# Beginnings of two attention stages: constant semaphores split, weight waits moved to their readers, bias tables loaded through SyncE's queue

## The reference

```
xn = _layernorm(x)
x = x + _L0_attn_ref(xn, ...) + _L0_ffn_ref(xn, ...)
xn = _layernorm(x)
x = x + _L1_attn_ref(xn, ...) + _L1_ffn_ref(xn, ...)
```

## Time and profile before

| | us |
|---|---|
| median of 3 runs | 2233.71 |
| their range | 2226.56 to 2234.21 |
| the profiled execution's own time | 2224.04 |
| its span, first to last instruction | 2222.4 |
| layer 0's attention, about | 0 to 500 |
| layer 0's feed-forward, about | 500 to 1263 |
| layer 1's attention begins | 1268.6 |

### The profile page before, as it was taken

One profiled execution on the slowest core, in us unless ns is written; L12 is line 12 of the kernel. 1 busy time (PEld: TensorE's weight loads), 2 busy tenths in 40 slices (PEclk: granted clock), 3 DMA queues, 4 the chain that ended last, 5 costly groups with the idle time before them and its releaser, 6 DMA issues. The chain is left out here.

```text
span 2222.4 us, 33910 instructions
## 1 busy us (share of the span) xinstructions
PE 1757.2 (79%) x10759; PEld 1099.7 (49%) x10759; DVE 1127.4 (51%) x2401; ACT 1024.4 (46%) x1356; POOL 1007.0 (45%) x778
## 2 busy tenths in 40 slices
PE   3889889870599999999999738877888888747933
PEld 2455555540487787787787513333433433235510
DVE  4666666537513313313313248877787788447211
ACT  1555555543313322223223118887787888713400
POOL 2443444430234344333433308777687777724212
PEclk8999999985799999999999868999998999969965
DMA  3333333306201101101100153222222222043989
GB/s 103 96 96 94 96 95 91 95 11 211 77 1 47 47 0 47 47 0 47 35 12 28 57 198 93 69 71 71 81 67 76 85 63 52 10 177 141 357 306 329
DMA packets 129732, 204.38 MB, mean 92 GB/s; under 512 B 14303, under 2 KB 84063, under 8 KB 129668
## 3 DMA queue, kind: packets, MB, share of 16 engines
q1 hardware_dynamic: 107896, 163.40, 24.7%
q10 hardware_dynamic: 16096, 20.65, 2.6%
q0 software_dynamic: 5680, 19.57, 2.3%
HBM read 95.96 MB, written 56.69 MB: 69 GB/s over the span
## 5 line engine op out<-in xcount | busy, mean ns | idle before, releaser
L773 POOL TENSOR_TENSOR l_prob<-l_prob,l_bias 128x1024 f32<-128x1024 f32 x192 | 452.3, 2376 | 145.5 <-ACT l_prob L881 144.6
L1336 POOL TENSOR_TENSOR f_hl<-f_full,f_hh 128x512 fp32r<-128x512 f32 x192 | 248.1, 1292 | 439.4 <-DVE f_hh L1378 282.9
L946 DVE CUSTOM_DVE_ANT_0 l_slot<-l_slot,l_bias 128x512 f32<-128x512 f32 x512 | 340.4, 714 | 51.5 <-PE l_slot L1020 50.4
L1378 DVE CAST f_hh<-f_full 128x512 fp32r<-128x512 f32 x128 | 74.9, 585 | 397.7 <-ACT f_full L1357 396.2
L884 ACT ACTIVATE l_prob<-l_prob 128x1024 f32<-128x1024 f32 x256 | 271.0, 1070 | 0.0
L1422 PE MATMUL f_ps<-f_hh,f_hi_h 128*128 128x512 f32 x1024 | 267.1, 397 | 0.0
L1432 PE MATMUL f_ps<-f_hl,f_hi_h 128*128 128x512 f32 x1024 | 265.8, 396 | 0.0
L451 DVE TENSOR_REDUCE l_peak<-l_slot 128x2 f32<-128x256 f32 (+3 forms) x256 | 206.3, 821 | 110.8 <-PE l_slot L535 108.5
L1357 ACT ACTIVATE f_full<-f_ps,f_h_s 128x512 f32<-128x512 f32 x128 | 86.4, 688 | 332.5 <-PE f_ps L1432 308.7
L376 ACT ACTIVATE l_prob<-l_slot 128x1024 f32<-128x1024 f32 (+3 forms) x256 | 174.7, 706 | 95.0 <-PE l_slot L554 91.9
L1422 PEld LDWEIGHTS f_ps<-f_hh,f_hi_h 128*128 128x128 f32 x1024 | 192.8, 188 | 49.3 <-ACT f_hh L1350 2.6
(11 more groups left out here) (211 smaller groups left out, 2655.0 us busy)
## 6 DMA issues: line engine op xcount, KB each, us to landing
l_stacks<-l_parts SPq DMA_DIRECT2D x384, 128.0 KB, 2.7
inter<-e_stage POOLq DMA_DIRECT2D x32, 512.0 KB, 5.1
c_rows<-inter SPq DMA_DIRECT2D x32, 512.0 KB, 9.7
attn<-l_out_sb ACTq DMA_DIRECT2D x16, 512.0 KB, 2.8
f_raw<-in_L_ffn_h_w SPq DMA_DIRECT2D x16, 512.0 KB, 3.3
e_w<-in_L_ffn_f SPq DMA_DIRECT2D x32, 256.0 KB, 4.8
l_bias<-ext ACTq DMA_DIRECT2D x16, 448.0 KB, 12.3
l_x_in<-in_L_attn_x SPq DMA_DIRECT2D x8, 512.0 KB, 3.8
```

What stands on the lines that cost most here:

```text
L773: return eng.tensor_tensor(probs(n), src, bias[:, h:h + 2, j * P:j * P + T], ALU.add)
L946: ins = dve.tensor_tensor_reduce(src, src, bias[:, 4 * g + 2 * pr + a, t * P:t * P + T], 1.0, 3 * NEG, ALU.add, ALU.max, peak[:, g, a, pr, ...
L1336: pool.tensor_tensor(hl[layer % 2][:, o], full[:, n % 2], hh[layer % 2][:, o].bitcast(F32), ALU.subtract).then_inc(h_lo.sem, 1)
```

## The change

In layer 0 `consts_in` counts only `power` and `ident`; `cols` and `half` count on a new `masks_in`, their loads stand behind those of the weights c, q and k; `wo` gets its own semaphore. POOL and PE wait at their start only for `power` and `ident`. PE waits for weight parts at the events that read them (2 at `latent`, 4 at `qk`, 5 at `v`, 6 at `out`), for `half_b` at the first score and for the ones at the first value. ACT rounds c, q and k first, then copies `half`; v and o are rounded behind the second `qk_copy`, and their low parts stand on DVE behind the second `qk_high`.

Layer 1 is treated in the same way (q and k first; v and o rounded behind the second `x_turn`, their low parts behind the fourth `qk`). Its bias loads go from ACT's queue to SP's: groups 0 and 1 (8 loads) behind the `keyed` load at the start, group 2 behind `stack` 1 and group 3 behind `stack` 2, each 4 loads. The number of loads and of instructions on DVE, PE and POOL stays as it was.

```diff
-        consts_in, w_in = sem("consts_in", unit=16), {n: sem(f"w_in_{n}", unit=16) for n in names}
+        consts_in, masks_in = sem("consts_in", unit=16), sem("masks_in", unit=16)
+        w_in = {n: sem(f"w_in_{n}", unit=16) for n in names + ("o",)}
...
-                for dst, src in ((power, c["c_pow"]), (ident, c["c_ident"]), (cols, c["c_cols"]), (half, c["c_half"])):
+                for dst, src in ((power, c["c_pow"]), (ident, c["c_ident"])):
                     sp.dma_start(dst[:], src).then_inc(consts_in.sem, 16)
-                for name in ("c", "q", "k", "v"):
+                for name in ("c", "q", "k"):
                     for dst, src in w["place"](name, raw[name], dict(w["loads"])[name]):
                         sp.dma_start(dst, src).then_inc(w_in[name].sem, 16)
-                sp.dma_start(raw_wo[:], w["wo"].rearrange("(k p) n -> p k n", p=P)).then_inc(consts_in.sem, 16)
+                for dst, src in ((cols, c["c_cols"]), (half, c["c_half"])):
+                    sp.dma_start(dst[:], src).then_inc(masks_in.sem, 16)
+                for dst, src in w["place"]("v", raw["v"], dict(w["loads"])["v"]):
+                    sp.dma_start(dst, src).then_inc(w_in["v"].sem, 16)
+                sp.dma_start(raw_wo[:], w["wo"].rearrange("(k p) n -> p k n", p=P)).then_inc(w_in["o"].sem, 16)
...
-                pool.wait_ge(consts_in.sem, 16 * 5)
+                pool.wait_ge(consts_in.sem, 16 * 2)
...
-                act.wait_ge(consts_in.sem, 16 * 5)
-                act.copy(half_b[:], half[:]).then_inc(half_ready.sem, 1)
...
-                act.wait_ge(w_in["v"].sem, 16 * 2)
-                rounded(wv[:, 0], raw["v"][:, 0])
-                rounded(wo[:, 0], raw_wo[:])
+                act.wait_ge(masks_in.sem, 16 * 2)
+                act.copy(half_b[:], half[:]).then_inc(half_ready.sem, 1)
+
+                def more_high_weights():
+                    act.wait_ge(w_in["v"].sem, 16 * 2)
+                    rounded(wv[:, 0], raw["v"][:, 0])
+                    act.wait_ge(w_in["o"].sem, 16)
+                    rounded(wo[:, 0], raw_wo[:])
...
+                        if n == 1 and opening(b):
+                            more_high_weights()
...
+                        if opening(b):
+                            dve.wait_ge(masks_in.sem, 16 * 2)
...
+                        if n == 1 and opening(b):
+                            more_low_weights()
...
+                        if opening(b):
+                            pe.wait_ge(w_ready.sem, 2)
...
+                        if opening(b):
+                            pe.wait_ge(w_ready.sem, 4)
...
+                        if n == 0 and opening(b):
+                            pe.wait_ge(half_ready.sem, 1)
...
+                        if opening(b):
+                            pe.wait_ge(w_ready.sem, 6)
...
-                pe.wait_ge(consts_in.sem, 16 * 5)
-                pe.wait_ge(w_ready.sem, 6)
-                pe.wait_ge(half_ready.sem, 1)
-                pe.wait_ge(ones_ready.sem, 2)
+                pe.wait_ge(consts_in.sem, 16 * 2)
...
+                def load_bias(g):
+                    for h in range(4 * g, 4 * g + 4):
+                        rising = bass.AP(w["ext"].tensor, w["ext"].offset + h * 2 * T, [[1, P], [1, UW]])
+                        sp.dma_start(bias[:, h], rising).then_inc(bias_in[g].sem, 16)
...
+                        if n in (1, 2) and opening(b):
+                            load_bias(n + 1)
...
-                sp.dma_start(raw["o"], w["wo"].rearrange("(k p) n -> p k n", p=P)).then_inc(consts_in.sem, 16)
+                sp.dma_start(raw["o"], w["wo"].rearrange("(k p) n -> p k n", p=P)).then_inc(w_in["o"].sem, 16)
                 sp.wait_ge(blank.sem, 3)
                 sp.dma_start(stacks[HROWS - 1:P:HROWS, 1].bitcast(F32), minus).then_inc(keyed.sem, 16)
+                for g in range(2):
+                    load_bias(g)
...
-                pool.wait_ge(consts_in.sem, 16 * 3)
+                pool.wait_ge(consts_in.sem, 16 * 2)
...
-                for h in range(H):
-                    rising = bass.AP(w["ext"].tensor, w["ext"].offset + h * 2 * T, [[1, P], [1, UW]])
-                    act.dma_start(bias[:, h], rising).then_inc(bias_in[h // 4].sem, 16)
-                def high_weights():
-                    for name, dst in (("q", wq), ("k", wk), ("v", wv)):
+                def high_weights(names):
+                    for name in names:
                         act.wait_ge(w_in[name].sem, 16)
-                        act.activation(dst[:, 0], raw[name], ACT.Copy, scale=HD ** -0.5 if name == "k" else 1.0)\
-                           .then_inc(w_high.sem, 1)
-                    act.wait_ge(consts_in.sem, 16 * 3)
-                    act.copy(wo[:, 0], raw["o"]).then_inc(w_high.sem, 1)
+                        act.activation({"q": wq, "k": wk, "v": wv, "o": wo}[name][:, 0], raw[name], ACT.Copy,
+                                       scale=HD ** -0.5 if name == "k" else 1.0).then_inc(w_high.sem, 1)
...
-                            high_weights()
+                            high_weights("qk")
...
+                        if n == KD - 1 and opening(b):
+                            high_weights("vo")
...
+                def low_weights(which):
+                    for m, (name, dst) in list(enumerate((("q", wq), ("k", wk), ("v", wv), ("o", wo))))[which]:
...
-                            low_weights()
+                            low_weights(slice(0, 2))
...
+                        if n == 3 and opening(b):
+                            low_weights(slice(2, 4))
...
+                        if opening(b):
+                            pe.wait_ge(w_ready.sem, 2)
...
+                        if opening(b):
+                            pe.wait_ge(w_ready.sem, 3)
...
-                pe.wait_ge(consts_in.sem, 16 * 3)
-                pe.wait_ge(w_ready.sem, 4)
-                pe.wait_ge(ones_ready.sem, 2)
+                pe.wait_ge(consts_in.sem, 16 * 2)
```

More of the change, by code:

```diff
@@ L644, in biased_attention @@
         single, o_bank = (ctx.enter_context(nc.psum_tensor(f"l1_{n}", [P, T], F32)) for n in ("single", "o_bank"))
-        consts_in, w_in = sem("consts_in", unit=16), {n: sem(f"w_in_{n}", unit=16) for n in names}
+        consts_in, w_in = sem("consts_in", unit=16), {n: sem(f"w_in_{n}", unit=16) for n in names + ("o",)}
         bias_in = [sem(f"bias_in{g}", unit=16) for g in range(QUADS)]
@@ L904, in _ @@
             def _(dve):
-                def low_weights():
-                    for m, (name, dst) in enumerate((("q", wq), ("k", wk), ("v", wv), ("o", wo))):
+                def low_weights(which):
+                    for m, (name, dst) in list(enumerate((("q", wq), ("k", wk), ("v", wv), ("o", wo))))[which]:
                         dve.wait_ge(w_high.sem, m + 1)
```

7 lines of the change are left out of this document (added).

## The result

| | before | changed |
|---|---|---|
| median of the runs (us) | 2232.07 (2222.91 to 2236.64, 8 runs) | 2216.89 (2214.36 to 2221.76, 8 runs) |
| the profiled execution's own time | 2224.04 | 2216.53 |
| its span | 2222.4 | 2214.9 |

The ratio is 0.9938, 95% interval 0.9919 to 0.9958: 13.8 us faster, where 14.3 was forecast, and 2216.89 against 2218.

What follows compares the result with a forecast made beforehand. Waits at both attention beginnings, where PE idles, were taken to bound what the change touches. 3.9 (layer 0) + 14.9 (layer 1) - 4.5 (x) = 14.3 us faster; forecast 2218 us, between 2209.7 and 2219.4, range 2208 to 2229.

Steps and rivals of the forecast that it cites:

- What bounds it: Both attention beginnings: PE idle, POOL held by the load of `wo`, PE by its low part; page averages say nothing.
- Layer 0, 3.9 us: Layer 0's beginning: `rstd` 1.5 us earlier and no 2.4 us wait for low parts, first transpose 3.9 us earlier.
- Layer 1, 14.9 us: Layer 1's beginning: `rstd` no longer waits behind bias loads and `wo`; PE's transposes start 14.9 us earlier.
- From the transposes to the maxima: Layer 1, first transpose to first score maxima: chain up to the stacks unchanged, so all moves forward by 14.9 us.
- Rival 3: PE's 2.4 GHz clock returns later against the work and takes some back: gain 8 to 11 us, about 2224; 20%.
- just fit: Layer 1: low parts of v and o, about 1.3 us, fit DVE's 1.52 us idle before the maxima, else cost tenths.
- The wait for x, 4.5 us: Layer 1: four bias loads ahead of batch 1's x in SP's queue delay it, 4.5 us lost.
- Rival 2: x late by issue time only (2.9 us), or waiting partly in another gap: 16 to 18 us gained, 2215; 12%.
- Layer 1's sum: Layer 1's terms: 14.9 us gained at the transposes less 4.5 lost to x; with layer 0's 3.9, 14.3 us.
- Rival 4: SP's one queue too slow for tables and stacks; at 152 GB/s the kernel is 11 us slower, 2245; 4%.
- Rival 5: Beginning not shortened as said: x or `ident` late, or a new wait; gain 3 to 8 us, about 2228; 9%.
- its last clause: A new wait takes the old one's place: low part of k before `xl`, or `bias_in` before the first maxima.

Runs made afterwards that it cites:

- after_again: The changed kernel once more, no edit: median 2220.09 us, ratio 0.9954 to the kernel before.
- l1_only: Layer 1 from the changed kernel, layer 0 from the kernel before: median 2222.08 us, ratio 0.9961 to the kernel before.
- x_first: The changed kernel with layer 1's bias group 2 behind the load of batch 1's x, not ahead: median 2211.00 us, ratio 0.9908 to the kernel before.
- x_early: The changed kernel with batch 1's x loaded ahead of batch 0's stack loads in both layers: 2210.69 us, ratio 0.9902 to the kernel before; repeat 2211.62, 0.9924.
- act_queue: The changed kernel with layer 1's 16 bias loads back on ACT's queue: median 2216.41 us, ratio 0.9930 to the kernel before.
- eight_ahead: The changed kernel with bias groups 2 and 3, eight loads, ahead of batch 1's x in layer 1: median 2221.91 us, ratio 0.9966 to the kernel before.
- wo_only: Layer 0 as changed; layer 1 as before except that `wo` has its own semaphore: median 2220.04 us, ratio 0.9963 to the kernel before.
- l0_only: Layer 0 from the changed kernel, layer 1 from the kernel before: median 2226.31 us, ratio 0.9983 to the kernel before.
- before_again: The kernel before against itself, no edit: median 2230.22 us, ratio 1.0003.
- x_early_warm: x_early with unread filler matmuls ahead of PE's first wait, six in layer 0, seven in layer 1: median 2204.00 us, ratio 0.9880 to the kernel before.
- pe_warm: The changed kernel with eight unread filler matmuls ahead of PE's first wait in layer 1: median 2216.85 us, ratio 0.9945 to the kernel before.

## Why the prediction was right, point by point

**What bounds it.** Right: PE's first matmul in each layer was held by a semaphore that also counted the load of `wo`, and by a wait for the low part of `wo` placed ahead of everything. Removing these moved both beginnings without moving any average of the page.

**Layer 0, 3.9 us.** The first transpose came 3.63 earlier, `rstd` at 8.62 (8.5 forecast), the first maxima at 34.25 (34.6), and the layer alone measured 3.8. The low parts of v and o did fit in front of the maxima.

**Layer 1, 14.9 us.** The first transpose came 14.95 earlier. `rstd` at 1274.75 and the transpose at 1278.24 are each 2.3 us later than forecast in absolute time, because layer 1 itself began at 1267.07 and not at 1268.59 less 3.9. That missing 2.4 us was lost in layer 0's later batches. The changed kernel copied the output of the fourth batch 4.08 us ahead of the kernel before (298.30 against 302.38), that of the fifth 2.46 ahead (355.04 against 357.50) and the last 1.53 (497.11 against 498.64). In the last part it was lost at PE: windows of 20 us of the changed kernel, and of the kernel before over about the same work:

```profile
...
436.00:456.00 20.00, 16.62 (x168) 9.55 (x169) 10.67 (x18) 10.57 (x15) 6.69 (x12) 0.91 0.18 41
```

```profile
...
440.00:460.00 20.00, 16.60 (x175) 10.74 (x174) 11.13 (x17) 11.19 (x15) 6.74 (x12) 1.00 0.17 39
```

In the same time PE got through 168 matmuls at a granted clock of 0.91, and 175 at 1.00. Among kernels whose layer 0 is the same program, its last output is copied anywhere between 492.4 and 498.7 us. A scatter of this size is enough for one pair of profiles to show 7.5 us and the medians 12: a single profile doesn't settle a few microseconds of total.

**From the transposes to the maxima, forecast as unchanged.** This step failed in size. The maxima gained 12.78 (46.19 to 33.41) where the transpose had gained 14.95. Rival 3's mechanism took 2.6 us, and 0.4 came back behind it. In all eight kernels with layer 1's changed waits and no filler (changed, after_again, l1_only, x_first, x_early twice, act_queue and eight_ahead), and in wo_only as well, the first three of layer 1's four products ran at 1.2 GHz; in the kernel before, l0_only and before_again it was the first one, one and two. So it is no luck of one run, and each slow product costs 1.26 us. Why the level of 2.4 GHz comes back only then is not shown. Every one of the nine had its first transpose earlier than the other three, but in x_early_warm too three products were slow, although its filler had kept PE busy up to 0.54 us before the transposes.

The low parts of v and o, which were to "just fit", took part too. Rows of the changed kernel, from its timeline at 1298 us, and below them the one of the kernel before that answers to the first:

```profile
...
1298.75 0.98 PE L1057 MATMUL l_slot<-l_stacks 63*128 63x512 f32 x6 [0.74 <-DMA l_stacks<-l_parts]
...
1299.88 0.68 DVE L939 SCALAR_TENSOR_TENSOR l_wo<-l_prob,l_wo 128x512 fp32r<-128x512 f32 x1
```

```profile
...
1313.74 0.97 PE L1020 MATMUL l_slot<-l_stacks 63*128 63x512 f32 x6 [1.82 <-DMA l_stacks<-l_parts]
```

And of after_again, whose layer 1 begins at 1261.92:

```profile
...
1292.92 0.97 PE L1057 MATMUL l_slot<-l_stacks 63*128 63x512 f32 x6
...
1295.32 0.69 DVE L979 CUSTOM_DVE_ANT_0 l_slot<-l_slot,l_bias 128x512 f32<-128x512 f32 x1
```

Before, the maxima started 0.07 us behind PE's first scores (1314.78 in the earlier trace rows less 1314.71): the stacks came last. Now it is 0.75 (1300.48 less 1299.73), and DVE goes without a gap from the low part of `wo` to the maxima: the low parts come last. after_again shows it plainly. Its scores start 0.68 us earlier from the block's start than in the changed kernel (31.00 for 31.68), and its maxima at 33.40, where it is 33.41. From the start of the fourth product to the maxima it was 4.53 us (1310.25 to 1314.78) and is 4.10 (1296.38 to 1300.48), so this part lost nothing against the kernel before, but by the rows of the two kernels 0.7 and 1.4 us more could have been won without the low parts in front (an estimate: 0.75 and 1.43 us behind the first scores, less the old 0.07). The whole 2.60 us that the four products take more (13.04 from first to fourth, where it was 10.44) less these 0.43 are the 2.17 measured.

The clock also varies later, from run to run. Windows from layer 1's first load to the copy of its first output, of the changed kernel and of its repeat:

```profile
...
1267.07:1443.10 176.03, 119.47 (x617) 57.35 (x619) 127.85 (x339) 107.00 (x130) 99.79 (x43) 0.80 0.44 133
```

```profile
...
1261.92:1441.30 179.38, 123.92 (x617) 60.30 (x619) 128.23 (x339) 107.02 (x130) 99.68 (x43) 0.77 0.43 130
```

The same 617 matmuls took 4.5 us more of PE at a lower granted clock, and the stretch was 3.4 us longer, after beginnings that agree within 0.2 us. The Trainium skill, TensorE: Matmul & The Clock Gate, section "What's actually happening", has the moment of the change vary from run to run. These traces agree for the long stretches and for the beginning before (one slow product in one profile of the same program, two in the other), and not for the changed beginning, where it was three in eight kernels.

**The wait for x, 4.5 us.** Right in mechanism, a quarter short: 5.81 (1.16 to 6.97). The term took the data at 406 GB/s, a rate from a stretch with nothing but stores, and the issue as wholly overlapped. The trace has x issued 1.40 us later behind the first maxima (2.11 for 0.71) and landing 4.4 us later behind its issue (8.8 for 4.4), at 311 GB/s in between; which of the two assumptions failed is not parted, as said above. Rival 2, issue time alone, is excluded: that is 2.03 us. Here the Trainium skill's sentence on issuers (DMA: Bandwidth & Descriptors, "Issuing engines are not separate DMA queues"), by which a second issuer saves only issue time, describes one side. ACT's issues did cost the 3.3 us that act_queue shows, but the place in the queue cost 5.8.

**Layer 1's sum.** 14.95 - 2.17 - 5.81 = 6.97, and the statistics of x came 51.35 - 44.38 = 6.97 earlier. With layer 0's 3.46 (43.12 to 39.66) that is 10.4 by the profiled pair, where 14.3 was forecast; the medians gave 13.8 and 10.3. The forecast was 2 us too high by the mean. That the first measurement, 13.8, lies so near to 14.3 is in part luck: the two terms that were left out or too small, 2.2 and 1.3 us, both make the gain smaller, and the rows of the beginnings carry only 10.4. The interval of 13.8 goes from 9.4 to 18.1 and holds both.

**Rival 4, a queue too slow.** Excluded. The tables and stores ahead of the stacks were over before them; the first stacks went out at 1291.96 into a nearly empty queue. Window of the changed kernel:

```profile
...
1290.00:1292.00 2.00, 0.58 (x2) 0.00 (x0) 0.69 (x1) 0.59 (x1) 0.00 (x0) 0.50 0.22 88
```

PE's wait for the first stacks, 0.74 us, was shorter than before. **Rival 5** is excluded by the two fences of the result: `ident` and x were there in time, and the first transposes came as early as forecast. In a small way its last clause came true, with another row: DVE's low parts now stand last before the first maxima of layer 1.

## What to carry to other kernels

A wait belongs at the instruction that reads the data, and a semaphore should count only what its waiters read: one weight load counted among constants held POOL for 12.7 us. Parting it brought the first matmul 4.8 of the 14.95 us, and moving the waits to their readers 6.8 more. A transfer moved to another queue should be read by what it then stands in front of: with four loads ahead of the next input it was waited for 7.0 us, with the same four behind it not at all. When a beginning is to be judged, follow it to the first event that every later one depends on (here batch 1's statistics), and test each part of the edit alone; the total of one pair of profiles hides a few microseconds in the clock.

## What was not expected of the hardware

- Full DMA engines (share 0.98 to 1.07) moved anything from 261 to 401 GB/s in these windows. The low rates stand where stack loads ran beside tables and x; that the mixture is the reason is a reading, not a test.
- SP issued a load of a table in 0.51 to 0.59 us (2.03 / 4, 4.68 / 8), but in 0.81 where the DMA engines were full (group 3 of the changed kernel, 3.24 us for four from 1308.64 on). ACT took 0.76 (12.12 / 16).
- The same program took 492.4 to 498.7 us to its last output of layer 0, at granted clocks that differed in single windows (0.91 and 1.00). That is as large as most edits here.
- Almost the same filler held PE at 2.4 GHz in one kernel and not in the other. In pe_warm it ran right up to the transposes, in x_early_warm it ended 0.54 us before them; whether that decided isn't shown.
